# First expert layer as three split products, both slots masked in one instruction, rounding on ScalarE

## The chip, the cores and the metric

The kernel runs on one core of a Trainium2 chip. The metric is the device time of one execution in microseconds (us); of several runs the median counts. The engines are TensorE (PE, matrix products), VectorE (DVE), ScalarE (ACT), GpSimd (POOL) and the DMA queues of SyncE (SP). Each engine works through its own instructions in the order in which they are written; semaphores are all that ties the engines together.

## The reference

Two transformer layers on x of 16 x 128 tokens with 128 features. The first has an attention by autocorrelation and a feed-forward part with composed weights; the second has a plain attention and a mixture of experts. Only the last part is touched by the change:

```
for _ in range(2):                                   # NUM_ITER
    ctx = concat([integrated, v])                    # 256 features
    shared_ctrl = gelu(ctx @ w_s1 + b_s1) @ w_s2 + b_s2
    # each token has K = 2 of E = 8 experts (its slots), with weights flat_w
    hidden = gelu(ctx @ expert_w1[e] + b1[e]);  ctrl = hidden @ expert_w2[e] + b2[e]
    # ctrl -> alpha = sigmoid, beta = softplus, gate = sigmoid; v, x from them
    x_next, v_next = shared weight * shared + rest * sum over the slots
    integrated += sigmoid(halt(x_next)) * refine(x_next) * integration_weight;  v = v_next
```

In the first pass v is zero, so that only the upper half of w1 counts and alpha isn't needed.

## The kernel before

Everything is kept transposed, features on the partitions and 2048 tokens in four chunks of 512 (CH). `build` writes the order of every engine by hand. After the composed weights comes a pipelined stretch of six slots (loop over `t in range(SLOTS)`, on each engine) for feed-forward, attention and router. Its last slot already holds step 0 of the last part: `hidden(0)`, and the masks of its tiles on DVE beside `route(3)`.

Then come eight steps, s = 0 to 7: chunk s % 4, first pass for s < 4, second pass from 4 on. A step has these parts:

- PE, loop at line 1309: `hidden(s+1)` (line 1141), `refine_b(s-2)`, `controls(s, GATE)` and `controls(s, BETA)`, in the second pass ALPHA ahead of them, and `refine_a(s-1)`. In the first pass refine_a comes after BETA, in the second between GATE and BETA. In step 0 the expert numbers (`expand`) and slot weights (`expand_weights`) of chunk 3 are spread through PE too.
- `hidden` makes four tiles of two experts each (128 rows) and the shared tile, as full fp32 products; one product each in the first pass, two (x and v) in the second. The five tiles alternate between two PSUM banks, so tile j waits for the gelu of tile j-2.
- ACT, loop at line 507: `hidden_gelus(s+1)` (line 418), `refine2(s-2)`, then `squashed` (line 495), which is a tanh of 1536 columns for ALPHA and GATE and a softplus for BETA, and `refine1(s-1)` (line 476): two gelus of 512 columns and one of 32 rows. `refine_a` needs the first of these before its 32-column product (`wh1`).
- DVE, loop at line 944: `stepped(s-1)` (line 894), which waits for the softplus of step s-1, `refine(s-2)` (line 928), `hidden_masked(s+1)` (line 761) and `shared_halves(s+1)`.

`hidden_masked` keeps of each tile the columns of the tokens whose slot has that expert, and splits the result in two fp32r halves for the products of `controls`. There are seven masked tiles: the first pair of experts once (`(0, None)`: only one slot can have each of them), and three pairs once for each of the two slots. Per tile it does, on DVE:

```
dve.scalar_tensor_tensor(hm[i % 2], idx[:, c, k, :], W("tile_expert", j, j + 1), hid[:, j, :],
                         ALU.is_equal, ALU.mult)                                  # kept
dve.tensor_copy(out[:, 0, i, :], hm[i % 2])                                       # upper, to fp32r
dve.tensor_tensor(out[:, 1, i, :], hm[i % 2], out[:, 0, i, :].bitcast(F), ALU.subtract)   # lower
```

`controls` is made of fp32r products: upper weights x upper half, lower weights x upper half, upper weights x lower half. The three control parts of the two slots and the shared one fill three of six PSUM banks; the next group but one waits for `squashed`.

Of the kernel before, what the change touches and what calls it, by code (L numbers as in the profile page):

```python
# [1421 lines left out]
```

## Time and profile before

| | before |
|---|---|
| median of 3 runs | 427.25 us (426.93 to 429.09) |
| the profiled execution | 426.0 us, its span 424.2 us |
| PE busy | 354.1 us, 83% |
| DVE busy | 296.2 us, 70% |
| ACT busy | 165.1 us, 39% |
| mean granted clock of PE | 0.947 |
| PE in the chain that ended last | 64% |

The span runs from the first to the last instruction. Times in the rows below are us from its start. A line number of a PE product is that of the helper `mm` (964); the tile names tell which product it is: `xi,pB` and `a,pB` are `hidden` (x and v), `hm_odd,ew_hi` and the like are `controls`, `zz,pB` is `refine_a` and `refine_b`, with `128*32` for its 32-column product. Names of tiles that share memory go by the memory: `zz` is also fh, xn and h1, `kv` is bg, ne and th, `b` is al, `ctxT` is r1, rr and hs, `wz` is hm.

### The profile page before, as it was taken

How to read it: one execution, taken by the hardware profiler on the slowest of the kernel's cores; microseconds unless marked ns; L12 is line 12 of the kernel's file. 1: busy time of each engine (PE TensorE's matmuls, PEld its weight loads, DVE VectorE, ACT ScalarE, POOL GpSimd, SP SyncE). 2: the span in 40 equal slices, each digit the busy share in tenths (PEclk: the TensorE clock that was granted, in tenths of full speed). 3: DMA queues.
4: the chain of work that ended last, by engine and by line, in shares of the span. 5: the costliest groups of instructions: out<-in, count | busy, mean ns of one | idle time of the engine just before them, and what ended most of it. 6: DMA issues, size and time to landing. Idle time of an engine off the chain costs nothing.

```text
span 424.2 us, 4164 instructions
## 1 busy us (share of the span) xinstructions
PE 354.1 (83%) x1406; PEld 207.6 (49%) x1406; DVE 296.2 (70%) x688; ACT 165.1 (39%) x231; POOL 17.0 (4%) x22
## 2 busy tenths in 40 slices
PE   4999997288886684799979899899999999998924
PEld 4646864154553342374626437347537536665511
DVE  0738527757675759998997949939489587866282
ACT  2401226247544465135362533522531452434511
POOL 0200101001100000000000000000000000000000
PEclk9989999879998899699989999999999999999958
DMA  8999230000000000000000000000000000000001
GB/s 268 429 361 300 82 130 0 1 2 0 0 2 0 0 2 0 1 0 2 0 1 2 1 0 0 2 0 0 0 2 1 0 0 26 0 2 25 0 7 42
DMA packets 10724, 17.92 MB, mean 42 GB/s; under 512 B 336, under 2 KB 8528, under 8 KB 9424
## 3 DMA queue, kind: packets, MB, share of 16 engines
q1 hardware_dynamic: 10704, 17.66, 12.2%
q8 instruction: 11, 0.18, 0.2%
q14 instruction: 9, 0.07, 0.1%
HBM read 16.61 MB, written 1.05 MB: 42 GB/s over the span
## 4 chain that ended last, share of the span: by engine, by line
PE 64%; DVE 17%; issue 10%; ACT 5%; POOL 2%; DMA 1%; POOLq 0%; SPq 0%; ACTq 0%; DVEq 0%
PE ps L964 60%; DVE zz L670 3%; DVE lst L655 2%; POOL lrs L319 2%; DMA ctxT<-in_ctxT 1%; PE ps L1047 1%; ACT zz L481 1%; PE ps L1035 1%; DVE hB L759 1%; ACT ctxT L428 1%; DVE st L555 1%; ACT kv L502 1%; DVE lmv L658 1%; DVE a L571 1%; ACT L481 0%
## 5 line engine op out<-in xcount | busy, mean ns | idle before, releaser
L964 PE MATMUL ps<-zz,pB 128*128 128x512 f32 (+2 forms) x96 | 48.8, 624 | 22.3 <-DVE ctxT L933 8.6
L964 PE MATMUL ps<-xi,pB 128*128 128x512 f32 (+1 forms) x88 | 49.6, 672 | 8.2 <-ACT hid L423 4.2
L964 PE MATMUL ps<-hm_even,ew_hi 128*128 128x512 f32 (+1 forms) x160 | 49.1, 418 | 0.0
L964 PE MATMUL ps<-hm_odd,ew_hi 128*128 128x512 f32 (+1 forms) x160 | 48.9, 417 | 0.0
L773 DVE SCALAR_TENSOR_TENSOR wz<-ring,pB,hid 128x512 f32<-128x512 bf16 x56 | 39.8, 746 | 0.3 <-issue 0.2
L964 PEld LDWEIGHTS ps<-zz,pB 128*128 128x128 f32 (+2 forms) x96 | 15.4, 180 | 50.0 <-issue 24.4
L964 PEld LDWEIGHTS ps<-xi,pB 128*128 128x128 f32 (+1 forms) x88 | 15.8, 197 | 32.3 <-ACT hid L423 14.2
L423 ACT ACTIVATE hid<-ps,pB 128x512 f32<-128x512 f32 x32 | 21.8, 687 | 21.6 <-PE ps L964 19.3
L964 PEld LDWEIGHTS ps<-hm_even,ew_hi 128*128 128x128 f32 (+1 forms) x160 | 26.9, 192 | 5.0
L964 PEld LDWEIGHTS ps<-hm_odd,ew_hi 128*128 128x128 f32 (+1 forms) x160 | 26.4, 188 | 5.4
L964 PE MATMUL ps<-hm_even,ew_lo 128*128 128x512 f32 (+1 forms) x80 | 27.6, 393 | 0.0
L964 PE MATMUL ps<-hm_odd,ew_lo 128*128 128x512 f32 (+1 forms) x80 | 27.6, 393 | 0.0
L505 ACT ACTIVATE kv<-ps 128x1536 f32<-128x1536 f32 x8 | 11.6, 1454 | 39.9 <-PE ps L964 39.9
L908 DVE TENSOR_TENSOR kv<-kv 128x1536 f32<-128x1536 f32 x4 | 7.0, 1759 | 28.4 <-ACT kv L502 28.4
L502 ACT ACTIVATE kv<-ps 128x1536 f32<-128x1536 f32 x8 | 11.6, 1452 | 29.3 <-PE ps L964 29.3
L670 DVE TENSOR_SCALAR zz<-ps,lmv,lrs 128x128 f32<-128x128 f32 x48 | 16.4, 404 | 8.4 <-POOL lrs L319 8.2
L655 DVE BATCH_NORM_STATS2 lst<-ps 128x6 f32<-128x128 f32 x48 | 10.7, 285 | 15.6 <-PE ps L1035 15.6
L933 DVE TENSOR_SCALAR ctxT<-ps,pB,iwh 128x512 f32<-128x512 f32 x8 | 6.5, 808 | 20.9 <-PE ps L964 20.9
L964 PE MATMUL ps<-a,pB 128*128 128x512 f32 x40 | 20.4, 592 | 0.0
L783 DVE TENSOR_TENSOR hm_odd<-wz,hm_odd 128x512 fp32r<-128x512 f32 x28 | 18.2, 687 | 0.1
L783 DVE TENSOR_TENSOR hm_even<-wz,hm_even 128x512 fp32r<-128x512 f32 x28 | 18.2, 686 | 0.1
L319 POOL TENSOR_TENSOR lrs<-lve,mhalf 128x4 f32<-128x4 f32 x12 | 12.1, 1007 | 120.8 <-DVE lve L660 120.8
(217 smaller groups left out, 614.3 us busy)
## 6 DMA issues: line engine op xcount, KB each, us to landing
ring<-in_fc1b SPq DMA_DIRECT2D x4, 1024.0 KB, 16.9
ring<-in_fc2a SPq DMA_DIRECT2D x4, 1024.0 KB, 10.0
ring<-in_packC SPq DMA_DIRECT2D x1, 1344.0 KB, 5.7
pB<-in_packB SPq DMA_DIRECT2D x1, 1078.5 KB, 9.9
ctxT<-in_ctxT SPq DMA_DIRECT2D x2, 512.0 KB, 6.4
xtok<-in_xtok SPq DMA_DIRECT2D x1, 1024.0 KB, 9.0
xT<-in_xT SPq DMA_DIRECT2D x1, 1024.0 KB, 11.0
a<-in_fc1a SPq DMA_DIRECT2D x1, 1024.0 KB, 12.9
```

The costliest lines, as they stand in the source:

```text
L319: pool.tensor_tensor(lrs[:, n % 2, :], lve[:, n % 2, :], mhalf[:, 0:BPC], ALU.pow)\
L423: act.activation(hid[:, j, :], hid_bank(s, j), ACT.Gelu, bias=W("eb1", j, j + 1)).then_inc(sem("hid"), 1)
L428: act.activation(hs, hid_bank(s, HT), ACT.Gelu, bias=W("bs1")).then_inc(sem("hs"), 1)
L502: act.activation(bg[:, 0], group_ps(n), ACT.Softplus).then_inc(sem("squash"), 1)
L505: act.activation(out, group_ps(n), ACT.Tanh, scale=0.5).then_inc(sem("squash"), 1)
L655: dve.bn_stats(lst[:, n % 2, j, :], t[:, j * D:(j + 1) * D]).then_inc(sem("lst"), 1)
L670: dve.tensor_scalar(ztok[:, n % 2, j, :], t[:, j * D:(j + 1) * D], lmv[:, n % 2, j, 0:1], lrs[:, n % 2, j:j + 1], ALU.subtract, ALU.mult)\
L773: dve.scalar_tensor_tensor(hm[i % 2], idx[:, c, 2 if k is None else k, :], W("tile_expert", j, j + 1), hid[:, j, :], ALU.is_equal, ALU.mul ...
L783: dve.tensor_tensor(out[:, 1, i, :], hm[i % 2], out[:, 0, i, :].bitcast(F), ALU.subtract).then_inc(sem("hlo"), 1)
L908: link(dve.tensor_tensor(bg[:, 0], bg[:, 0], thrice(ne), ALU.mult))
L933: dve.tensor_scalar(rr, bank[7], W("bf2"), iwh[:, 0:1], ALU.add, ALU.mult).then_inc(sem("rr"), 1)
L964: return pe.matmul(out, lhsT, rhs, start=start, stop=stop)
```

## The change

- `hidden`: each full fp32 product becomes three fp32r products (upper weights x upper state, lower weights x upper state, upper weights x lower state). The halves of w1 are made once in the pipelined stretch, `w1x_hi` on ACT (slot 1), `w1x_lo` on DVE (slot 2). The halves of the state, x and in the second pass v too, are made per step: `state_upper` on ACT, `state_lower` on DVE.
- `hidden_masked`: both slots of tiles 1 to 3 are masked in one instruction of 1024 columns, and their lower halves are made in one of 1024 columns; tile 0 is masked in place, in two instructions of 64 partitions. The copies to fp32r (`upper`) go from DVE to ACT.
- ACT's order: `upper(s+1, ...)` and `state_upper(s+2)` stand between the `squashed` calls of step s, and `upper(0, ...)` and `state_upper(1)` in the last slot ahead of `r1_gelu`.
- `slot_masks` works on the two slots' numbers without copying them first.
- Some tiles move: al, hs, the second hm buffer; w1 stands first in pack B.

The diff, without the lines that only place tiles:

```diff
@@ -419,13 +433,34 @@
...
             if s >= 1:
-                act.wait_ge(sem("hm"), NT * (s - 1) + 2 * j + 1)
+                act.wait_ge(sem("hm") if j else sem("hlo"), HT * (s - 1) + j + 1)
             act.activation(hid[:, j, :], hid_bank(s, j), ACT.Gelu,
...
         act.activation(hs, hid_bank(s, HT), ACT.Gelu, bias=W("bs1")).then_inc(sem("hs"), 1)
+    def upper(s, tiles):
+        for j in tiles:
+            act.wait_ge(sem("hm"), HT * s + j + 1)
+            if s >= 2:
+                act.wait_ge(sem("part_ps"), group(s - 1, 0))
+            out = masked(s)[:, 0, 2 * j - 1:2 * j + 1, :] if j else masked(s)[:, 0, 0, :]
+            act.activation(out, hm[j % 2] if j else hid[:, 0, :], ACT.Copy).then_inc(sem("hhi"), 1)
+    def state_upper(s):
+        c = s % NCH
+        act.wait_ge(sem("hid_ps"), 5 * s)
+        if s >= NCH:
+            act.wait_ge(sem("xi"), c + 1)
+        act.activation(x_hi, xi[:, ck(c)], ACT.Copy).then_inc(sem("xhi"), 1)
+        if s >= NCH:
+            act.wait_ge(sem("v1"), c + 1)
+            act.activation(v_hi, vT[:, ck(c)], ACT.Copy).then_inc(sem("vhi"), 1)
     z_ffn(0)
@@ -460,6 +495,8 @@
...
             act.activation(swc[:, 0:1], W("sw"), ACT.Exp, scale=-1.0).then_inc(sem("swe"), 1)
+            act.activation(w1x_hi, pB[:, colB["ew1"][1]:colB["ew1"][1] + W1C], ACT.Copy)\
+                .then_inc(sem("w1x_hi"), 1)
         if x:
@@ -468,10 +505,18 @@
...
             ln_evac("rt", t - 2, xi[:, ck(t - 2)])
+        if t == 2:
+            act.wait_ge(sem("z"), LN["rt", 0] + 1)
+            act.wait_ge(sem("bp"), 2)
+            act.activation(x_hi, xi[:, ck(0)], ACT.Copy).then_inc(sem("xhi"), 1)
+        if t == SLOTS - 1:
+            upper(0, (0, 1))
+            state_upper(1)
+            upper(0, (2,))
         if q:
...
     second_exp(NCH - 1)
+    upper(0, (3,))
     def refine1(s):
@@ -509,16 +554,24 @@
...
             refine2(s - 2)
+        squashed(s, parts(s)[0])
+        if s + 1 < STEPS:
+            upper(s + 1, (0, 1))
+        if s == 0:
+            expand_evac(NCH - 1, 7, 6)
+        if s + 2 < STEPS:
+            state_upper(s + 2)
+        if s + 1 < STEPS:
+            upper(s + 1, (2,))
+        if s >= NCH:
+            squashed(s, GATE)
+        if s + 1 < STEPS:
+            upper(s + 1, (3,))
         if s < NCH:
-            squashed(s, GATE)
-            if s == 0:
-                expand_evac(NCH - 1, 7, 6)
             squashed(s, BETA)
...
         else:
-            squashed(s, ALPHA)
-            squashed(s, GATE)
             refine1(s - 1)
@@ -747,50 +800,71 @@
...
         dve.wait_ge(sem("idx"), 2 * c + 2)
-        dve.tensor_copy(idx[0:64, c, 2, :], idx[0:64, c, 0, :]).then_inc(sem("idt"), 1)
-        dve.tensor_copy(idx[64:128, c, 2, :], idx[64:128, c, 1, :]).then_inc(sem("idt"), 1)
-        dve.wait_ge(sem("idt"), 2 * c + 2)
-        dve.tensor_scalar(m72[:, ck(c)], idx[:, c, 2, :], W("bias_expert"), None, ALU.is_equal)\
-            .then_inc(sem("m72"), 1)
+        for k in range(2):
+            p = slice(64 * k, 64 * k + 64)
+            dve.tensor_scalar(m72[p, ck(c)], idx[p, c, k, :], W("bias_expert")[p], None, ALU.is_equal)\
+                .then_inc(sem("m72"), 1)
     def slot_weights(c, ba, bb):
...
             dve.tensor_copy(cb[:, c, k, :], bank[(ba, bb)[k]][:, :]).then_inc(sem("cb"), 1)
-    def hidden_masked(s, tiles):
+    def kept(s, j):
         c = s % NCH
+        dve.wait_ge(sem("hid"), HT * s + j + 1)
+        if j == 0:
+            dve.wait_ge(sem("idx"), 2 * (c + 1))
+            for k in range(2):
+                p = slice(64 * k, 64 * k + 64)
+                dve.scalar_tensor_tensor(hid[p, 0, :], idx[p, c, k, :], W("tile_expert", 0, 1)[p],
+                                         hid[p, 0, :], ALU.is_equal, ALU.mult)\
+                    .then_inc(sem("hm" if k else "hm_half"), 1)
+        else:
+            if s >= 1 or j == 3:
+                dve.wait_ge(sem("hlo"), HT * s + (0, -1, 2)[j - 1])
+            dve.scalar_tensor_tensor(hm[j % 2], idx[:, c, :, :], W("tile_expert", j, j + 1),
+                                     hid[:, j, :].unsqueeze(1).to_broadcast([128, 2, CH]),
+                                     ALU.is_equal, ALU.mult).then_inc(sem("hm"), 1)
+    def lower(s, j):
         out = masked(s)
-        n0 = NT * s
-        def kept(i):
-            j, k = TILES[i]
-            dve.wait_ge(sem("hid"), HT * s + j + 1)
-            if n0 + i >= 2:
-                dve.wait_ge(sem("hlo"), n0 + i - 1)
-            dve.scalar_tensor_tensor(hm[i % 2], idx[:, c, 2 if k is None else k, :],
-                                     W("tile_expert", j, j + 1), hid[:, j, :],
-                                     ALU.is_equal, ALU.mult).then_inc(sem("hm"), 1)
-        def upper(i):
-            dve.wait_ge(sem("hm"), n0 + i + 1)
-            dve.tensor_copy(out[:, 0, i, :], hm[i % 2]).then_inc(sem("hhi"), 1)
-        def lower(i):
-            dve.wait_ge(sem("hhi"), n0 + i + 1)
-            dve.tensor_tensor(out[:, 1, i, :], hm[i % 2], out[:, 0, i, :].bitcast(F),
-                              ALU.subtract).then_inc(sem("hlo"), 1)
-        if tiles[0] == 0:
-            dve.wait_ge(sem("idt"), 2 * (c + 1))
-            if s >= 2:
-                dve.wait_ge(sem("part_ps"), group(s - 1, 0))
-        for stage in (kept, upper, lower):
-            for i in tiles:
-                stage(i)
+        dve.wait_ge(sem("hhi"), HT * s + j + 1)
+        if j:
+            i = slice(2 * j - 1, 2 * j + 1)
+            dve.tensor_tensor(out[:, 1, i, :], hm[j % 2], out[:, 0, i, :].bitcast(F), ALU.subtract)\
+                .then_inc(sem("hlo"), 1)
+        else:
+            dve.wait_ge(sem("hm_half"), s + 1)
+            dve.tensor_tensor(out[:, 1, 0, :], hid[:, 0, :], out[:, 0, 0, :].bitcast(F), ALU.subtract)\
+                .then_inc(sem("hlo"), 1)
+    def state_lower(s):
+        c = s % NCH
+        dve.wait_ge(sem("xhi"), s + 1)
+        dve.tensor_tensor(x_lo, xi[:, ck(c)], x_hi.bitcast(F), ALU.subtract).then_inc(sem("xlo"), 1)
+        if s >= NCH:
+            dve.wait_ge(sem("vhi"), c + 1)
+            dve.tensor_tensor(v_lo, vT[:, ck(c)], v_hi.bitcast(F), ALU.subtract)\
+                .then_inc(sem("vlo"), 1)
+    def hidden_masked(s, next_state):
+        kept(s, 0)
+        kept(s, 1)
+        kept(s, 2)
+        if next_state:
+            state_lower(s + 1)
+        lower(s, 0)
+        lower(s, 1)
+        kept(s, 3)
+        lower(s, 2)
+        shared_halves(s)
+        lower(s, 3)
     def shared_halves(s):
@@ -871,24 +945,34 @@
...
             shared_share()
+            dve.wait_ge(sem("w1x_hi"), 1)
+            dve.tensor_tensor(w1x_lo, pB[:, colB["ew1"][1]:colB["ew1"][1] + W1C],
+                              w1x_hi.bitcast(F), ALU.subtract).then_inc(sem("w1x_lo"), 1)
         if a:
...
             slot_weights(t - 3, 2, 3)
+        if t == 3:
+            state_lower(0)
         if f:
...
         if t == SLOTS - 1:
-            hidden_masked(0, (0,))
-            hidden_masked(0, (1, 2))
+            kept(0, 0)
+            kept(0, 1)
+            kept(0, 2)
+            lower(0, 0)
+            lower(0, 1)
         if q:
...
             ln_scale("att", t)
-    hidden_masked(0, (3, 4))
+    state_lower(1)
+    kept(0, 3)
+    lower(0, 2)
     weigh(NCH - 1)
-    hidden_masked(0, (5, 6))
     shared_halves(0)
+    lower(0, 3)
     dve.wait_ge(sem("consts"), 2)
@@ -947,9 +1031,7 @@
...
         if s + 1 < STEPS:
-            for tiles in ((0,), (1, 2), (3, 4), (5, 6)):
-                hidden_masked(s + 1, tiles)
-            shared_halves(s + 1)
+            hidden_masked(s + 1, s + 2 < STEPS)
         if s == 0:
@@ -1141,12 +1223,12 @@
...
         c, it2 = s % NCH, s >= NCH
+        pe.wait_ge(sem("w1x_lo"), 1)
+        pe.wait_ge(sem("xlo"), s + 1)
         if it2:
-            pe.wait_ge(sem("xi"), c + 1)
-            pe.wait_ge(sem("v1"), c + 1)
+            pe.wait_ge(sem("vlo"), c + 1)
         for j in range(HT + 1):
-            name, wd = ("ew1", E * H) if j < HT else ("ws1", 2 * H)
-            o = j * 128 if j < HT else 0
+            o, wd = (j * 128, E * H) if j < HT else (2 * E * H, 2 * H)
             if j >= 2:
@@ -1157,9 +1239,15 @@
...
                     pe.wait_ge(sem("h1"), s - 2)
-            last = mm(hid_bank(s, j), W(name, o, o + 128), xi[:, ck(c)], stop=not it2)
+            out, w = hid_bank(s, j), slice(o, o + 128)
+            mm(out, w1x_hi[:, w], x_hi, stop=False)
+            mm(out, w1x_lo[:, w], x_hi, start=False, stop=False)
+            last = mm(out, w1x_hi[:, w], x_lo, start=False, stop=not it2)
             if it2:
-                last = mm(hid_bank(s, j), W(name, wd + o, wd + o + 128), vT[:, ck(c)], start=False)
+                w = slice(o + wd, o + wd + 128)
+                mm(out, w1x_hi[:, w], v_hi, start=False, stop=False)
+                mm(out, w1x_lo[:, w], v_hi, start=False, stop=False)
+                last = mm(out, w1x_hi[:, w], v_lo, start=False)
             last.then_inc(sem("hid_ps"), 1)
@@ -1256,9 +1344,9 @@
...
             pe.wait_ge(sem("squash"), n - 1)
-        pe.wait_ge(sem("m72"), c + 1)
+        pe.wait_ge(sem("m72"), 2 * (c + 1))
         pe.wait_ge(sem("hsl"), s + 1)
-        pe.wait_ge(sem("hlo"), NT * s + 1)
+        pe.wait_ge(sem("hlo"), HT * s + 1)
         w_hi, w_lo = weights(ew2_hi, 0), weights(ew2_lo, 0)
@@ -1273,7 +1361,7 @@
...
             j, k = TILES[i]
-            pe.wait_ge(sem("hlo"), NT * s + i + 1)
+            pe.wait_ge(sem("hlo"), HT * s + j + 1)
             out = hi if k else lo
```

## Rows read from the trace of the kernel before

**Rows 1.** The page: busy us, share and instructions; granted clock in 40 slices of 10.6 us

```profile
PE 354.1 (83%) x1406; PEld 207.6 (49%) x1406; DVE 296.2 (70%) x688; ACT 165.1 (39%) x231; POOL 17.0 (4%) x22
PEclk9989999879998899699989999999999999999958
```

**Rows 2.** Timeline of PE, step 3: start us, us, line, out<-in, count [idle before]

```profile
257.31 0.39 PE L964 MATMUL ps<-hm_odd,ew_lo 128*128 128x512 f32 x1
...
258.01 0.40 PE L964 MATMUL ps<-hm_odd,ew_lo 128*128 128x512 f32 x1
...
270.38 1.05 PE L964 MATMUL ps<-zz,pB 128*32 128x512 f32 x2 [1.83 <-ACT zz L481]
...
272.31 1.02 PE L964 MATMUL ps<-a,pB 128*128 128x512 f32 x2
273.17 1.02 PE L964 MATMUL ps<-xi,pB 128*128 128x512 f32 x2
```

**Rows 3.** Timeline of ACT, step 3

```profile
260.78 1.46 ACT L505 ACTIVATE kv<-ps 128x1536 f32<-128x1536 f32 x1 [5.42 <-PE ps L964]
262.25 1.28 ACT L502 ACT_TABLE_LOAD   x1
266.87 1.45 ACT L502 ACTIVATE kv<-ps 128x1536 f32<-128x1536 f32 x1 [3.33 <-PE ps L964]
268.34 1.28 ACT L481 ACT_TABLE_LOAD   x1
269.64 1.26 ACT L481 ACTIVATE zz<-ps,pB 128x512 f32<-128x512 f32 x2
```

**Rows 4.** Timeline, step 5: ALPHA's tanh, refine1, the product that waits

```profile
324.22 1.45 ACT L505 ACTIVATE b<-ps 128x1536 f32<-128x1536 f32 x1 [5.41 <-PE ps L964]
...
331.67 1.26 ACT L481 ACTIVATE zz<-ps,pB 128x512 f32<-128x512 f32 x2
...
332.41 1.04 PE L964 MATMUL ps<-zz,pB 128*32 128x512 f32 x2 [0.40 <-ACT zz L481]
```

**Rows 5.** Groups of instructions: busy us, mean ns of one | idle before it

```profile
L423 ACT ACTIVATE hid<-ps,pB 128x512 f32<-128x512 f32 x32 | 21.8, 687 | 21.6 <-PE ps L964 19.3 <-DVE wz L773 2.3
L779 DVE CAST hm_odd<-wz 128x512 fp32r<-128x512 f32 x28 | 10.8, 422 | 0.1
L919 DVE SCALAR_TENSOR_TENSOR kv<-kv,swc 128x1024 f32<-128x1024 f32 x4 | 5.1, 1285 | 0.1
L917 DVE TENSOR_TENSOR kv<-kv,hB 128x1024 f32<-128x1024 f32 x4 | 4.9, 1225 | 0.1
L783 DVE TENSOR_TENSOR hm_odd<-wz,hm_odd 128x512 fp32r<-128x512 f32 x28 | 18.2, 687 | 0.1
L351 ACT ACTIVATE zz<-ps 128x512 f32<-128x512 f32 x4 | 2.4, 596 | 13.5 <-PE ps L1047 13.5
```

**Rows 6.** Timeline, step 0: ACT, DVE's slot weights, PE's hidden(2)

```profile
184.75 1.45 ACT L505 ACTIVATE kv<-ps 128x1536 f32<-128x1536 f32 x1 [7.00 <-PE ps L964]
186.10 1.08 ACT L415 ACTIVATE ring<-ps 128x512 bf16<-128x512 f32 x2
...
192.07 1.29 DVE L759 COPY hB<-ps 128x512 f32<-128x512 f32 x2 [1.44 <-PE ps L1137]
...
193.41 4.93 PE L964 MATMUL ps<-xi,pB 128*128 128x512 f32 x10 [0.95 <-DVE hB L759]
```

**Rows 7.** Timeline, slot 5: r1_gelu, start of route(3), first controls

```profile
161.15 0.68 ACT L400 ACTIVATE ctxT<-ps,pB 32x512 f32<-32x512 f32 x1 [1.14 <-PE ps L964]
...
164.81 0.18 DVE L714 COPY lg<-ps 128x32 f32<-128x32 f32 x1
...
177.07 0.39 PE L964 MATMUL ps<-xtok,bp_e 64*128 64x512 bf16 x2 [2.54 <-issue]
```

**Rows 8.** Timeline of PE at the end: the same six records twice

```profile
410.52 4.42 PE L964 MATMUL ps<-zz,pB 128*128 128x512 f32 x6 [8.56 <-DVE ctxT L933]
415.80 3.01 PE L964 MATMUL ps<-zz,pB 128*128 128x512 f32 x6 [0.86 <-ACT zz L486]
```

More of the change, by code:

```diff
@@ L33 @@
 VG = -(-B // VB)
-PACK_B = [("wq", 128, D), ("wo", 128, D), ("bq", 128, 1), ("bv", 128, 1), ("bo", 128, 1),
+PACK_B = [("ew1", 128, 2 * E * H), ("ws1", 128, 4 * H), ("wq", 128, D), ("wo", 128, D), ("bq", 128, 1), ("bv", 128, 1), ("bo", 128, 1),
           ("wr1", 128, 32), ("br1", 32, 1), ("wr2", 33, E), ("wh1", 128, 32), ("bh1", 32, 1),
-          ("wh2", 32, 1), ("bh2", 128, 1), ("ew1", 128, 2 * E * H), ("eb1", 128, HT),
-          ("ws1", 128, 4 * H), ("bs1", 128, 1), ("wf1", 128, 2 * D), ("bf1", 128, 2),
+          ("wh2", 32, 1), ("bh2", 128, 1), ("eb1", 128, HT), ("bs1", 128, 1), ("wf1", 128, 2 * D), ("bf1", 128, 2),
           ("wf2", 128, 2 * D), ("bf2", 128, 1), ("iw", 128, 1), ("mu", 128, 1), ("sw", 128, 1),
@@ L71, in sem @@
             return sems[name]
+        xtok_at = (nc.sbuf_base + 31) // 32 * 32
         xtok_f = sb("xtok", [128, B * D])
@@ L78, in build @@
         ctxT = sb("ctxT", [128, T])
+        pA_at = (nc.sbuf_base + 31) // 32 * 32
         pA = sb("pA", [128, nA])
+        pB_at = (nc.sbuf_base + 31) // 32 * 32
         pB = sb("pB", [128, nB])
         a1_f = sb("a1", [128, KC * D])
+        b2_at = (nc.sbuf_base + 31) // 32 * 32
         b2_f = sb("b2", [128, KC * D])
@@ L184, in C @@
             return ring[0:r, PC0 + at:PC0 + at + n]
-        idx = ring[:, IDX0:IDX0 + 3 * T // 2].bitcast(BF).rearrange("p (c a n) -> p c a n", c=NCH, a=3)
+        idx = ring[:, IDX0:IDX0 + T].bitcast(BF).rearrange("p (c a n) -> p c a n", c=NCH, a=2)
         m72 = xtok_f[:, 0:T // 2].bitcast(BF)
@@ L200, in build @@
         hid = hid_f[:, :].rearrange("p (f n) -> p f n", f=HT)
-        hs = ctxT[:, 2 * CH:3 * CH]
+        hs = wz[:, 2 * CH:3 * CH]
         hsh = sb("hsh", [128, 2, CH], FR)
-        hm = (wz[:, 0:CH], wz[:, CH:2 * CH])
+        hm = (wz[:, 0:2 * CH].rearrange("p (k n) -> p k n", k=2),
+              ring[:, IDX0 + T:IDX0 + T + 2 * CH].rearrange("p (k n) -> p k n", k=2))
         hm_even = sb("hm_even", [128, 2, NT, CH], FR)
@@ L209, in build, with placed @@
         ws2_lo = sb("ws2_lo", [128, 3 * D], FR)
+        W1C = 2 * E * H + 4 * H
+        def placed(name, cols, at):
+            return nc.alloc_sbuf_tensor_at(name, [128, cols], FR, offset=at)[:, :]
+        w1x_hi = placed("w1x_hi", W1C, b2_at)
+        w1x_lo = placed("w1x_lo", W1C, pB_at + 4 * colB["ew1"][1])
+        x_hi, x_lo = (placed(n, CH, xtok_at + 4 * (2 + i) * CH) for i, n in enumerate(("x_hi", "x_lo")))
+        v_hi, v_lo = placed("v_hi", CH, b2_at + 4 * W1C), placed("v_lo", CH, pA_at)
         bg = kv[:, 0:6 * CH].rearrange("p (a k n) -> p a k n", a=2, k=3)
@@ L213, in build @@
         th = kv[:, 7 * CH:8 * CH]
-        al = b2_f[:, 0:3 * CH].rearrange("p (k n) -> p k n", k=3)
+        al = ctxT[:, 0:3 * CH].rearrange("p (k n) -> p k n", k=3)
         fh = zz[:, 0:2 * CH].rearrange("p (f n) -> p f n", f=2)
```

## The prediction

> **What bounds the kernel now.** I read the page first: TensorE (PE) is busy 83% of the span, and its granted clock is low only in a few slices [rows 1]. The chain of waits gives PE 64% of the span. Then I read the timelines from 177 us on, where the eight steps of the last layer run. Step s issues, on PE, hidden(s+1), refine_b(s-2), one `controls` group per part, and refine_a(s-1) ahead of the last group (after it in steps 0 to 3). All of it is back to back, except for a short stop per step. In step 3 the GATE group ends near 260.75 and the BETA group at 266.8. PE finishes the first half of refine_a and stops for 1.83 us, until 270.38 [rows 2]. It waits there for ScalarE (ACT): softplus 266.87, table load, gelu 269.64 [rows 3]. The table load ahead of that softplus (262.25) costs nothing: it runs while PE does the BETA group. So a step is PE work plus a short tail through ACT. VectorE (DVE) makes the masked halves one step ahead and ends them before they are needed.
>
> **Gain on PE.** A full fp32 product is two records of 0.43 us start to start, 0.86 us together (272.31 to 273.17) [rows 2]. Three fp32r products take 258.01 - 257.31 = 0.70 us [rows 2]. So hidden() falls by 0.16 us per product set, 5 sets in steps of the first pass and 10 in those of the second: at most 4 x 0.8 + 4 x 1.6 = 9.6 us. It can't all be had: two PSUM banks alternate, so tile j waits for the gelu of tile j-2, 0.69 us each [rows 5].
> - hidden(2): five tiles at 0.86 took 4.87 before the next group. Now tiles 2 to 4 go at the gelu's pace, 4.0 in all: gain 0.87. hidden(3): 0.4, for its end waits for the last gelu.
> - hidden(4), hidden(5): 1.4 us a tile, start to refine_b 9.72 before, 7.95 after: 1.77 each.
> - hidden(6), hidden(7): the first gelu stands behind a softplus and a table load, so tile 2 starts at 3.7 us in both kernels; three tiles by 0.3: 0.92 each.
> Sum 6.65 us.
>
> **The copies on ScalarE, first pass (steps 1, 2, 3).** DVE loses seven casts of 0.42 us a step [rows 5] (and gets state_lower, 0.69 or 1.4), but DVE isn't the bound. What matters is the place of the copies in ACT's order. `upper(s+1)` stands between squashed(s, GATE) and squashed(s, BETA), and upper(s+1, 3) waits for kept(s+1, 3). That waits for lower(s+1, 1) (same buffer), which waits for upper(s+1, 1); and DVE has state_lower(s+2) in front of it, which waits for ACT's copy of the state. So ACT and DVE pass the work to and fro, and softplus is queued behind it. From the end of the GATE group, in us:
> - tanh done 1.5 [rows 3]; upper 0 (512 columns, 0.60) 2.1; upper 1 (1024 columns, halfway between the 596 ns of 512 and the 1.46 us of 1536, so 1.03) 3.15; x_hi 3.75 [rows 3, 5];
> - DVE: x_lo 0.69, lower 0 0.70, lower 1 (1024 columns, 1225 ns), kept 3 (1024 columns, 1285 ns), each with 0.03 to 0.1 between: 7.83 [rows 5];
> - ACT: upper 3 8.9, table load 1.28, softplus 1.46: 11.7; table load for gelu, gelu 0.69: 13.75.
> Before, the product behind that gelu started 270.38 - 260.75 = 9.63 us after the GATE group. The load that used to be free is exposed as well. Step 1: +4.1. Steps 2 and 3 make the state of the second pass, with v_lo (0.70) in the DVE part: +4.8 each. DVE's own kept 0 to 2 are done before the tanh ends, so they don't lengthen this.
>
> **Step 0.** Here hidden(2) waited for DVE's slot weights, 193.41 - 184.7 = 8.7 us after the GATE group [rows 6]. Now ACT has tanh, upper 0 and 1 (3.15), two index evictions (1.09) and x_hi before DVE can go on (4.85); DVE then has x_lo, lower 0, lower 1, kept 3, lower 2, shared halves (1.18), lower 3, the masks (0.65) and the slot weights (1.29): 14.55. That is +5.85.
>
> **Second pass (steps 4 to 6).** From the end of ALPHA: tanh 1.5, upper 0 and 1 3.15, x_hi 3.75; DVE x_lo, v_lo, lower 0, lower 1, kept 3: 8.5; upper 3 9.6; gelu of refine1 10.3. Before, that gelu released PE at 332.41 - 324.18 = 8.23 [rows 4]. So +2.1 in steps 4 and 5. Step 6 makes no state: kept 3 at 5.8, the GATE tanh done at 7.55, upper 3 8.6, gelu 9.3: +1.1. Step 7 has no masked work: 0. BETA's table load stays behind refine1, where it was.
>
> **Prologue.** Slot 2 puts w1x_lo (1280 columns, 1.5 us by the slope of DVE's rows) and slot 3 x_lo (0.7) on DVE; part goes into its idle time, and the index copies left out give a little back: I take 0.9. ACT's copies of w1 and x stand where it waits for PE anyway: nothing, or 1.8 us if that cover were gone. In slot 5 r1_gelu, which ended at 161.83, comes after upper 0, upper 1, x_hi(1) and upper 2, and ends at 165.85; with router2's 1.0 behind it route(3) starts at 166.9, not 164.81 [rows 7]. It takes 2.85, then x_lo(1) 0.7: hidden(1) starts at 170.5. Upper(0, 3) is done at 172.8, the gelu load at 174.1, and the tiles go at the gelu's pace; the last ends at 177.2, or 178.7 at half the clock, in the middle 178.0. With the 0.9 the first group starts at 178.9, not 177.07 [rows 7]: +1.8. Bounds: -1, if DVE's shorter list tells in the end, and +4, if all of r1_gelu's delay stays.
>
> **The clock.** The tail's stop on PE grows from 1.83 to about 5.9 us in steps 1 to 3, and to 6.5 us in step 0. No row shows a stop of just that length. Where PE had stood idle for 8.6 us, six records took 4.42 us; the same six took 3.01 us five us later [rows 8], and the page's clock row falls to 5 in that slice [rows 1]: 1.2 GHz for part of it, against 2.4. After stops of 1.83 us the clock stays high in most steps. So I bound it: nothing, or 5.0 us a stop (12 us of PE work at the low clock before it is back); I take 2.0, near the row. Four stops, 8 us; the clock digit 8 in the slice of 212 to 223 says that the kernel before already pays about 2 us in hidden(3) [rows 1]. Net +6, bounds 0 and +18.
> The Trainium skill (TensorE: Matmul & The Clock Gate, What's actually happening) says of a model that it may leave the ramp out, as under 1% of a typical span. By it the sum would be without this term, the second rival below. The row of the 8.6 us stop speaks for a cost of 1.4 us each, so the sum keeps the term.
>
> **Sum.** 1.8 + 5.85 + 4.1 + 4.8 + 4.8 + 2.1 + 2.1 + 1.1 - 6.65 = +20.0, and the clock +6: +26. The profiled execution took 426.0 us with a span of 424.2, so it would take 452.0 with a span of 450. It lies 1.25 us under the median of the runs, 427.25; I predict 453.0 for the median.
>
> **Unknown costs.** ACT's copy of 1024 columns from SBUF has no row: not under 0.60 (512 columns), not over 1.46 (1536). Two stand in each chain (uppers 1 and 3): -0.9 to +0.9 a step. DVE's masked instruction of 1024 columns with a bf16 and a repeated operand: 0.75 (one of 512) to 1.76 (1536 columns), taken by the same form at 1024 (1285 ns): -0.5 to +0.5. Over seven steps -9.5 to +9.5 together at the ends.
>
> **Rivals.**
> 1. PE stays the bound (the other side): if ACT reached the copies early enough for kept 3 to be done within the 6.1 us of the last group, the tail would be hidden as now and only the 6.65 us of hidden() would show: 427.25 - 6.65 + 1.8 = 422.4. For it: ACT is busy 39% and DVE 70% of the span [rows 1], and the work moved is small. Against: the chain after the tanh is 7.4 us on two in-order engines, over 6.1; it decides only from a chain 1.3 us shorter, and then the table load would also have to go ahead of upper 3.
> 2. The tail grows, the clock holds through stops of 6 us: 427.25 + 20 = 447.
> 3. The tail grows, and the clock stays at 1.2 GHz for much of the first pass, 5 us lost at each of four stops: 427.25 + 20 + 18 = 465.
> 4. The tail grows by half of what I say, as when DVE and ACT copies come at the low ends: 427.25 + 10 + 2 = 439.
> 5. No change: the 6.65 us and a tail of that size cancel, 427.
>
> **Chances.** Forecast 0.50, rival 2 0.20, rival 3 0.08, rival 4 0.14, rival 1 0.05, rival 5 0.03. The range 440 to 463 holds the forecast, rival 2 and the near part of 4 and 3. A change of 0.5% (2.1 us) is about what a measurement here can tell. Faster 0.05, same 0.03, slower 0.92.
>
> **What would show it.** In the profile after, ACT's softplus in steps 1 to 3 stands right behind a copy of 1024 columns and a table load, 10 us and more after the tanh; the PE stop ahead of the 32-column product is near 6 us in steps 1 to 3 and near 2.6 in steps 4 and 5; hidden(4) goes from 9.7 to 8.0 us; the clock falls after the long stops. It is wrong if softplus still starts within 0.1 us of the BETA group's end, or if those stops stay under 3 us.

## The result and the profile after

| | before | after |
|---|---|---|
| median | 427.1 us (426.2 to 429.1, 4 runs) | 451.3 us (450.2 to 453.1, 4 runs) |
| ratio after to before, 95% interval | | 1.056 (1.051 to 1.061) |
| profiled execution, its span | 426.0, 424.2 us | 451.9, 450.0 us |
| mean granted clock of PE | 0.947 | 0.917 |
| PE in the chain that ended last | 64% | 52% |

The kernel is 24.2 us slower. The forecast was 453.0, and for the profiled execution 452.0 with a span of 450.

The page after, the same lines as in [rows 1], in slices of 11.25 us:

```profile
PE 353.3 (79%) x1466; PEld 225.6 (50%) x1466; DVE 287.3 (64%) x601; ACT 200.4 (45%) x276; POOL 17.0 (4%) x22
PEclk9999999699987895988969889979999999999968
PE 52%; DVE 22%; issue 11%; ACT 10%; POOL 2%; DMA 1%; POOLq 0%; ACTq 0%; SPq 0%; DVEq 0%
```

PE has as many busy microseconds as before, although its products became shorter: part of them ran at a lower clock. DVE has 9 us less work and ACT 35 us more, and neither is close to full. What is new is waiting.

Timeline of ACT in step 2 after (start us, us; the idle time ahead in brackets). It answers to [rows 3]; steps 1 and 3 have the same order (step 1 without the copy of v):

```profile
244.28 1.45 ACT L550 ACTIVATE kv<-ps 128x1536 f32<-128x1536 f32 x1 [5.31 <-PE ps L1046]
245.63 0.62 ACT L452 ACTIVATE hm_odd<-hid 128x512 fp32r<-128x512 f32 x1
246.15 1.05 ACT L452 ACTIVATE hm_odd<-ring 128x1024 fp32r<-128x1024 f32 x1
247.10 0.62 ACT L460 ACTIVATE x_hi<-xi 128x512 fp32r<-128x512 f32 x1
247.62 0.62 ACT L463 ACTIVATE v_hi<-a 128x512 fp32r<-128x512 f32 x1
248.14 1.05 ACT L452 ACTIVATE hm_odd<-wz 128x1024 fp32r<-128x1024 f32 x1
252.20 1.06 ACT L452 ACTIVATE hm_odd<-ring 128x1024 fp32r<-128x1024 f32 x1 [3.01 <-DVE ring L828]
253.28 1.28 ACT L547 ACT_TABLE_LOAD   x1
254.57 1.45 ACT L547 ACTIVATE kv<-ps 128x1536 f32<-128x1536 f32 x1
256.04 1.28 ACT L526 ACT_TABLE_LOAD   x1
257.34 1.27 ACT L526 ACTIVATE zz<-ps,pB 128x512 f32<-128x512 f32 x2
```

And DVE in the same stretch:

```profile
247.75 0.69 DVE L849 TENSOR_TENSOR x_lo<-xi,x_hi 128x512 fp32r<-128x512 f32 x1 [3.30 <-ACT x_hi L460]
248.36 0.68 DVE L852 TENSOR_TENSOR v_lo<-a,v_hi 128x512 fp32r<-128x512 f32 x1
248.96 0.68 DVE L842 TENSOR_TENSOR hm_odd<-hid,hm_odd 128x512 fp32r<-128x512 f32 x1
249.56 1.22 DVE L838 TENSOR_TENSOR hm_odd<-ring,hm_odd 128x1024 fp32r<-128x1024 f32 x1
250.89 1.28 DVE L828 SCALAR_TENSOR_TENSOR ring<-ring,pB,hid 128x1024 f32<-128x1024 bf16 x1
```

The ball goes over twice. DVE stands idle for 3.30 us until ACT has copied the state. Then ACT stands idle for 3.01 us until DVE has masked tile 3 (the instruction at 250.89). Only behind the last copy does ACT come to the softplus, and now the load of its table (253.28) stands on the path; in [rows 3] the same load was done 3.3 us ahead of its softplus, beside PE's work.

Timeline of PE behind that gelu, which answers to [rows 2]:

```profile
258.08 1.91 PE L1046 MATMUL ps<-zz,pB 128*32 128x512 f32 x2 [6.10 <-ACT zz L526]
...
260.51 0.63 PE L1046 MATMUL ps<-x_hi,w1x_lo 128*128 128x512 f32 x1
260.94 0.63 PE L1046 MATMUL ps<-x_lo,w1x_hi 128*128 128x512 f32 x1
...
265.20 0.40 PE L1046 MATMUL ps<-v_hi,w1x_lo 128*128 128x512 f32 x1
265.43 0.40 PE L1046 MATMUL ps<-v_lo,w1x_hi 128*128 128x512 f32 x1
```

The stop is 6.10 us instead of 1.83; in steps 1 and 3 it is 5.43 and 6.02. Behind it two products take 1.91 us, not 1.05 [rows 2], and the products of `hidden` start 0.43 us apart instead of 0.23: the lower of the clock's two levels (1.2 GHz against 2.4; the granted clock is 0.50 from 257 to 262 us and 1.00 from 264 on), until some 5 us after the stop.

Step 0, start of hidden(2), and the end of the kernel, which answer to [rows 6, 8]:

```profile
201.64 0.77 PE L1046 MATMUL ps<-x_hi,w1x_hi 128*128 128x512 f32 x1 [6.11 <-DVE hB L811]
...
322.40 1.05 PE L1046 MATMUL ps<-zz,pB 128*32 128x512 f32 x2 [1.92 <-ACT zz L526]
...
435.20 5.58 PE L1046 MATMUL ps<-zz,pB 128*128 128x512 f32 x6 [8.56 <-DVE ctxT L1017]
```

In step 0 PE stops for 6.11 us instead of 0.95. The first stop of the second pass (322.40) is 1.92 us; those behind it are 1.84 and 1.35, and all three were 0.40 [rows 4].

### The profile page after: what moved, and what is told of

Same layout as the page of the kernel before. It is cut to its first block, busy times and chain, and to the rows that moved or that the text cites. A ratio compares the mean times of both kernels' runs of the same rounds, so it can differ in the third digit from the quotient of the medians.

```text
span 450.0 us, 4256 instructions
## 1 busy us (share of the span) xinstructions
PE 353.3 (79%) x1466; PEld 225.6 (50%) x1466; DVE 287.3 (64%) x601; ACT 200.4 (45%) x276; POOL 17.0 (4%) x22
## 3 DMA queue, kind: packets, MB, share of 16 engines
HBM read 16.61 MB, written 1.05 MB: 39 GB/s over the span
## 4 chain that ended last, share of the span: by engine, by line
PE 52%; DVE 22%; issue 11%; ACT 10%; POOL 2%; DMA 1%; POOLq 0%; ACTq 0%; SPq 0%; DVEq 0%
PE ps L1046 49%; DVE zz L723 2%; DVE ring L828 2%; DVE lst L708 2%; POOL lrs L333 2%; ACT hm_even L452 2%; DVE hm_odd L838 1%; DMA ctxT<-in_ctxT 1%; ACT hm_odd L452 1%; PE ps L1129 1%; ACT zz L526 1%; ACT hid L437 1%; PE ps L1117 1%; ACT L526 1%; ACT L547 1%
## 5 line engine op out<-in xcount | busy, mean ns | idle before, releaser
L1046 PE MATMUL ps<-zz,pB 128*128 128x512 f32 (+2 forms) x96 | 52.5, 665 | 38.3 <-ACT zz L526 24.5
L1046 PE MATMUL ps<-x_hi,w1x_hi 128*128 128x512 f32 x40 | 20.2, 506 | 13.0 <-DVE hB L811 6.1
L550 ACT ACTIVATE kv<-ps 128x1536 f32<-128x1536 f32 x8 | 11.6, 1453 | 28.9 <-PE ps L1046 28.9
L1046 PEld LDWEIGHTS ps<-x_hi,w1x_hi 128*128 128x128 f32 x40 | 9.0, 225 | 24.3 <-issue 15.1
L828 DVE SCALAR_TENSOR_TENSOR ring<-ring,pB,hid 128x1024 f32<-128x1024 bf16 x16 | 20.5, 1283 | 1.0
L849 DVE TENSOR_TENSOR x_lo<-xi,x_hi 128x512 fp32r<-128x512 f32 x8 | 5.5, 691 | 24.3 <-ACT x_hi L460 24.2
L708 DVE BATCH_NORM_STATS2 lst<-ps 128x6 f32<-128x128 f32 x48 | 10.6, 284 | 15.4 <-PE ps L1117 15.3
L547 ACT ACTIVATE kv<-ps 128x1536 f32<-128x1536 f32 x8 | 11.6, 1452 | 16.3 <-PE ps L1046 16.3
L1046 PE MATMUL ps<-x_hi,w1x_lo 128*128 128x512 f32 x40 | 18.1, 451 | 0.0
L1046 PE MATMUL ps<-x_lo,w1x_hi 128*128 128x512 f32 x40 | 17.8, 446 | 0.0
```

Source lines behind the costliest of these rows:

```text
L547: act.activation(bg[:, 0], group_ps(n), ACT.Softplus).then_inc(sem("squash"), 1)
L550: act.activation(out, group_ps(n), ACT.Tanh, scale=0.5).then_inc(sem("squash"), 1)
L708: dve.bn_stats(lst[:, n % 2, j, :], t[:, j * D:(j + 1) * D]).then_inc(sem("lst"), 1)
L828: dve.scalar_tensor_tensor(hm[j % 2], idx[:, c, :, :], W("tile_expert", j, j + 1), hid[:, j, :].unsqueeze(1).to_broadcast([128, 2, CH]), A ...
L1046: return pe.matmul(out, lhsT, rhs, start=start, stop=stop)
```

## The experiments

The kernel before ran beside each, with a median of 427.3 us beside e1 to e4 and 427.2 beside e5 to e8. A ratio is to it, with its 95% interval. Where two kernels are compared that both differ from it by little (e1, e2, e5, e8), the uncertainties of both ratios count.

| what is run | median us | ratio | span, clock of the profile |
|---|---|---|---|
| e1: copies back on DVE | 425.7 | 0.994 (0.990 to 0.997) | 421.2, 0.943 |
| e3: one copy later in ACT's order | 431.9 | 1.012 (1.008 to 1.015) | 429.8, 0.934 |
| e4: full products again, copies on ACT | 444.4 | 1.037 (1.032 to 1.042) | 444.2, 0.930 |
| e8: wide masks alone | 426.1 | 0.997 (0.994 to 1.000) | 423.5, 0.952 |
| e2: e1 with masks per slot | 430.0 | 1.004 (1.001 to 1.007) | 429.0, 0.926 |
| e6: PE kept busy through the stops | 443.3 | 1.034 (1.028 to 1.041) | 442.4, 0.942 |
| e7: tanh in place of softplus | 439.7 | 1.026 (1.020 to 1.032) | 438.8, 0.916 |
| e5: copies on DVE, step 0 reordered | 421.9 | 0.988 (0.983 to 0.992) | 420.0, 0.944 |

### The copies back on DVE (e1)

```diff
-def upper(s, tiles):                          # on ACT, with state_upper, among the squashed calls
...
-    act.activation(out, hm[j % 2] if j else hid[:, 0, :], ACT.Copy)
+def upper(s, j):                              # on DVE, in hidden_masked, with state_upper
...
+    dve.tensor_copy(out, hm[j % 2] if j else hid[:, 0, :])
```

> The changed kernel with all copies to fp32r of the masked tiles and of the state on DVE again (ScalarE keeps only the one of w1). Theory (the tail of each step is ScalarE's copies and DVE's lowers passed to and fro ahead of softplus and of refine1's gelu): the tails go back to those before, PE's stops ahead of the 32-column product to 1.8 us in steps 1 to 3 and 0.4 in 4 to 6, the clock drops after them are gone, and the 6.65 us of hidden() show: 427 - 6.7 + 2 to 3 in the pipelined stretch = 423, 420 to 426. Rival (the split products or the double-width masks themselves cost the time, on PE or DVE): it stays near 450. Rival (DVE becomes the bound, for it gets 1.1 to 2.0 us more a step than in the kernel before): 430 to 435.

It took 425.7 us: all 24 us are gone, and 1.6 more. The product behind the gelu, in steps 1 to 3:

```profile
217.88 1.04 PE L1045 MATMUL ps<-zz,pB 128*32 128x512 f32 x2 [1.83 <-ACT zz L497]
242.74 1.04 PE L1045 MATMUL ps<-zz,pB 128*32 128x512 f32 x2 [1.83 <-ACT zz L497]
270.58 1.05 PE L1045 MATMUL ps<-zz,pB 128*32 128x512 f32 x2 [1.83 <-ACT zz L497]
```

The stop is again 1.83 us and the granted clock stays at 1.00 behind all three, with DVE busy 73% instead of 64%. So the whole loss goes when one part of the change is taken back, the move of the rounding to ACT.

### One copy later in ACT's order (e3)

```diff
-                if s + 1 < STEPS:
-                    upper(s + 1, (3,))
                 if s < NCH:
                     squashed(s, BETA)
-                    if s >= 1:
-                        refine1(s - 1)
-                else:
+                if s >= 1:
                     refine1(s - 1)
+                if s + 1 < STEPS:
+                    upper(s + 1, (3,))
+                if s >= NCH:
                     squashed(s, BETA)
```

> The changed kernel with one thing moved: upper(s+1, 3) stands behind squashed(s, BETA) and refine1(s-1) in the first pass, and behind refine1(s-1) in the second, with all the same work on ScalarE. Theory (the order, not the amount): tails of steps 1 to 6 go back to about the ones before; step 0 keeps some 3 us and the pipelined stretch its 3 us: 427 - 6.65 + 6 = 427, 423 to 432. Rival (the amount of work on ScalarE): 445 or more.

431.9 us: 19.4 of the 24.2 us come back, with the same work on ACT. ACT in step 2:

```profile
242.87 1.05 ACT L452 ACTIVATE hm_odd<-wz 128x1024 fp32r<-128x1024 f32 x1
243.94 1.28 ACT L547 ACT_TABLE_LOAD   x1
245.24 1.45 ACT L547 ACTIVATE kv<-ps 128x1536 f32<-128x1536 f32 x1
246.71 1.28 ACT L526 ACT_TABLE_LOAD   x1
248.00 1.27 ACT L526 ACTIVATE zz<-ps,pB 128x512 f32<-128x512 f32 x2
249.82 0.68 ACT L531 ACTIVATE zz<-ps,pB 32x512 f32<-32x512 f32 x1 [0.56 <-PE ps L1045]
250.41 1.04 ACT L452 ACTIVATE hm_odd<-ring 128x1024 fp32r<-128x1024 f32 x1
```

The copy that waited 3.01 us now stands behind refine1, and no stop of PE waits for it. The stops on PE are 1.82, 2.04 and 1.96 us, and 0.40 in the second pass. Only step 0 keeps its cost: hidden(2) still starts behind a stop of 6.11 us, at 201.39. There the expectation was off (3 us were to remain of the start), for of step 0 only upper(1, 3) was moved. The other copies still stand ahead of the index evictions and of x_hi, and DVE's slot weights behind x_lo.

### Full products with the copies on ACT (e4), and wide masks alone (e8)

```diff
...
-    mm(out, w1x_hi[:, w], x_hi, stop=False)
-    mm(out, w1x_lo[:, w], x_hi, start=False, stop=False)
-    last = mm(out, w1x_hi[:, w], x_lo, start=False, stop=not it2)
+    last = mm(hid_bank(s, j), W(name, o, o + 128), xi[:, ck(c)], stop=not it2)
...
```

and no `state_upper` or `state_lower`. e8 is e4 with the copies on DVE, as in e1: of the change it keeps only the new masks (1024 columns for tiles 1 to 3, tile 0 in place) and `slot_masks` without its copies.

> The changed kernel with hidden() made of full fp32 products as before; the halves of w1 and of the state aren't made. Masks, copies on ScalarE and their place stay. Theory: hidden() costs its 6.65 us again, but the chain of each tail is 1.1 us (x) or 1.7 to 2.2 us (x and v) shorter; the tail of steps 1 to 3 is still 2 to 3 us over the one before and PE's stop 4 to 4.5 us: 447, 441 to 451. Rival (the split products are what costs): back at 427.

> Only the double-width masks of the change: hidden() with full fp32 products, copies on DVE, no halves of w1 or of the state. Theory: DVE's work isn't on the path of the steps, and tile 0 in two instructions gives back what the width saves; only slot 5, where DVE is behind, can tell: 426, 424 to 428. Against e1_round_dve (425.7) it tells what the split products alone are worth there: hidden()'s 6.65 us less what their halves cost in slots 2 to 5 and in step 0. Rival: the masks' width is worth 3 us or more, and this one is at 423 or below.

e4 took 444.4. Without x_hi and v_hi on ACT and x_lo and v_lo on DVE the chain is 1.7 to 2.3 us shorter (stops of 3.70, 3.79 and 3.71 us), the stop ahead of hidden(2) is 3.32 us instead of 6.11, and the clock costs less behind them. Together that is worth more than the shorter products: the split products cost 6.9 us net in the order of the change (451.3 against 444.4).

e8 took 426.1, against 425.7 of e1. So the wide masks alone give about 1 us (by the interval 0.1 to 2.8), and the split products nothing that can be told in e1's order: there hidden(2) starts at 197.7 us and in e8 at 191.7. 3.7 of these 6.0 us are there at hidden(0) already (156.3 against 152.6, partly the clock, see e2); the other 2.3 come in slot 5 and step 0, where DVE makes the halves of the state ahead of the slot weights of chunk 3.

### Masks per slot (e2)

```diff
-dve.scalar_tensor_tensor(hm[j % 2], idx[:, c, :, :], ..., hid[:, j, :].unsqueeze(1).to_broadcast([128, 2, CH]), ...)
+for k in range(2):
+    dve.scalar_tensor_tensor(hm[j % 2][:, k, :], idx[:, c, k, :], ..., hid[:, j, :], ...)
```

The same for the copies and the lower halves.

> As e1_round_dve, but tiles 1 to 3 are masked, copied and lowered per slot in instructions of 512 columns (18 instead of 9 a step). By the durations a 1024-column mask saves 0.2 us against two of 512 start to start (1.20 against 1.32), all nine about 0.5 us a step, in DVE's slack: theory: same as e1 within 1 us (423). Rival (the width of the masks matters): 3 us or more over e1.

430.0, or 4.3 us over e1: the expectation of no difference was wrong. Not all of it can be placed. The two profiles lie 7.8 us apart. 2.7 of that is there at the start of hidden(0) already (159.0 against 156.3), and a kernel whose instructions up to there are those of "after" (e7) also starts it at 158.5, against 155.6 of "after": that much comes and goes with the granted clock before 155 us. In slot 5 and step 0, where PE waits for DVE, the shift grows by 1.6 us up to hidden(2), which waits 4.00 us instead of 3.15, and the clock falls behind it: 5.3 us at the product ahead of hidden(3). In e2 the clock falls once more behind the stop of 1.83 us in step 2, which adds 1.5, and the last 0.9 come at the last products. The tails of the steps are the same in both, 1.83 and 0.40 us. So only the 1.6 us, and the 1.0 of the clock behind them, stand where the narrower instructions are on the path; how much of the 4.3 us of the medians is theirs stays open.

### PE kept busy (e6)

```diff
+def keep_busy(n, count):
+    pe.wait_ge(sem("squash"), n + 1)
+    for _ in range(count):
+        mm(bank[3 * (n % 2)], onesb[:, 0:128], onesb[:, :])
```

Called ahead of the wait for the gelu in steps 1 to 3, and in step 0 ahead of hidden(2).

> The changed kernel with 24 bf16 products of 512 columns on PE, into a bank that is free, in the long stop of each of steps 0 to 3 (some 5.2 us of work in stops of 5.4 to 6.1 us); their results aren't used. Theory (the stops also cost clock): the granted clock stays at 2.4 GHz after them, the 32-column product takes 1.05 us for two records as before and not 1.92, hidden()'s products follow each other in 0.23 us and not 0.43: 2.0 to 2.6 us less per stop, four stops: 451.3 - 9 = 442, 440 to 445. Rival (the clock term is nothing, and the loss is all in the chain): 450 to 452.

443.3. PE in the stop of step 2, with the 24 unused products:

```profile
248.37 5.34 PE L1046 MATMUL ps<-onesb 128*128 128x512 bf16 x24
254.64 1.04 PE L1046 MATMUL ps<-zz,pB 128*32 128x512 f32 x2 [0.93 <-ACT zz L526]
255.61 0.50 PE L1046 MATMUL ps<-x_hi,w1x_hi 128*128 128x512 f32 x1
255.95 0.40 PE L1046 MATMUL ps<-x_hi,w1x_lo 128*128 128x512 f32 x1
256.19 0.40 PE L1046 MATMUL ps<-x_lo,w1x_hi 128*128 128x512 f32 x1
```

Nothing that the kernel needs comes sooner in the chain on ACT and DVE, but the two products take 1.04 us and those of `hidden` start 0.23 apart: the clock is high behind the stop. From the end of each stop to the end of its `hidden`, e6 takes 1.2, 2.3, 2.3 and 2.2 us less than the kernel after (hidden(2) to hidden(5)): 8.1 us for the clock behind the four stops. What else differs between the two profiles nearly cancels: in step 4 of e6 the clock falls behind a stop of 1.92 us, which costs 1.6, and the last products take 1.2 less. The medians lie 8.0 us apart, a third of the loss of 24.2; the rest is what the longer stops themselves and the prologue cost, less what the split products give.

### The tables (e7)

```diff
-act.activation(bg[:, 0], group_ps(n), ACT.Softplus)
+act.activation(bg[:, 0], group_ps(n), ACT.Tanh)
```

> The changed kernel with tanh in the place of softplus for BETA, which changes the values of beta. ScalarE then has no table load before it nor behind it. Theory (the load that was hidden now stands in the tail): in steps 1 to 3 both loads (1.28 us each) leave the chain of upper 3, load, softplus, load, gelu: PE's stop shrinks from 6 to 3.4 us, 2.6 us less each, and with shorter stops some of the clock's loss goes: 451.3 - 7.8 - 4 = 440, 435 to 444. In step 0 and the second pass nothing changes. Rival (the loads run beside the copies and cost nothing): 448 or more.

With tanh beta has other values, so only the time of this kernel is of use: 439.7, or 11.6 us less. In step 2 ACT goes on without a gap:

```profile
250.13 1.06 ACT L452 ACTIVATE hm_odd<-ring 128x1024 fp32r<-128x1024 f32 x1 [3.01 <-DVE ring L828]
251.09 1.43 ACT L547 ACTIVATE kv<-ps 128x1536 f32<-128x1536 f32 x1
252.42 1.26 ACT L526 ACTIVATE zz<-ps,pB 128x512 f32<-128x512 f32 x2
```

ACT still waits 3.01 us for DVE, and the stops shrink to 2.58, 3.26 and 3.18 us. Two loads of 1.28 us stand on the path of each of those steps in the kernel after; one of them did before. The loads also leave places that the expectation took as unchanged: the stop in step 7 goes from 1.82 to 0.40 us, and hidden(6) and hidden(7) are 1.0 us shorter each. The profile of e7 reaches the first tanh of step 0 3.0 us later than that of the kernel after, so it tells the differences only from there on.

### The version to keep (e5)

From e1, these calls moved in slot 5 and step 0:

```diff
+            if t == SLOTS - 1:                     # ACT: the copy of x for hidden(1)
+                act.wait_ge(sem("hid_ps"), 5)
+                act.activation(x_hi, xi[:, ck(1)], ACT.Copy).then_inc(sem("xhi"), 1)
...
-                    upper(0, 0)                    # DVE, slot 5: now behind route(3)
-                    upper(0, 1)
-                    lower(0, 0)
-                    lower(0, 1)
+                    state_lower(1)
...
+                if s == 1:                         # DVE, ahead of shared_halves(1)
+                    slot_masks(NCH - 1)
+                    slot_weights(NCH - 1, 7, 6)
```

and `shared_halves(0)` goes ahead, `weigh(3)` behind the lower halves.

> e1_round_dve with its slot 5 and step 0 put in another order: ScalarE makes x_hi(1) where it was idle, DVE does x_lo(1) and route(3) ahead of the upper and lower halves of step 0, shared_halves(0) ahead of tile 3, weigh(3) last, and slot masks and weights of chunk 3 stand ahead of shared_halves(1). In e1 PE stopped 7.6 us ahead of hidden(1) and 3.2 us ahead of hidden(2). Theory: e1 still has 4.3 us of the change's cost at the start of hidden(2) (197.7 against 193.4 in the kernel before), and it goes, with a little more: GATE of step 0 near 176, hidden(2) near 192: 425.7 - 5.7 = 420, 417 to 423, faster than both kernels. Rival: the pipelined stretch is bound by its clock and DVE in another place, and it stays at 424 to 427.

421.9 us, 5.2 under the kernel before beside it. Against e1 the medians differ by 3.7 us and the ratios by 2.6, with an interval that just reaches 0. hidden(2) starts at 194.8, not at 197.7 (192 was expected):

```profile
194.81 0.47 PE L1047 MATMUL ps<-x_hi,w1x_hi 128*128 128x512 f32 x1 [2.18 <-DVE hB L777]
```

Behind this stop the clock falls (from 195.4 to 198.9 us), which it doesn't in e1, so that the product ahead of hidden(3) is 2.0 us sooner than in e1. e5 beats both kernels, the one before by 0.8 to 1.7%. It is also 4.2 us under e8. But e8 has its slot 5 and step 0 in the old order, and no run has full products in the order of e5: how much of the 4.2 us the split products give and how much the order isn't shown.

## Why the prediction was right

The direction, the place and the mechanism hold: the copies among ACT's calls lengthen PE's stops, and e3 and e1 take that loss back. The sum lands within 2 us: 453.0 forecast, 451.3 measured; +26 forecast between the profiles, +25.8 measured. That it lands so near is partly luck, for its terms are off by up to 3.7 us and cancel. The steps one by one, from the starts of the same instructions in the two profiles:

- **The chain, steps 1 to 3.** Forecast +4.1, +4.8, +4.8; measured +3.6, +4.3, +4.2. In step 2 the GATE group ends near 244.25. Kept 3 is done 7.9 us later (8.5 by the terms with v_lo), upper 3 9.0, softplus 11.8, gelu 13.8 (9.6, 12.4, 14.4). The order is exactly the forecast one. The 0.6 us are in how the terms were added: I put 0.03 to 0.1 us between instructions of one engine, and behind one another they start 0.05 to 0.1 us before the earlier one's recorded end (ACT's copies of 0.62 and 1.05 us start 0.52 and 0.95 apart). The unknown cost was right: the copy of 1024 columns took 1.05 us (1.03 taken), the masked instruction 1.28 (1.285 taken). e3 is the test of the mechanism: one copy moved, 19.4 us back.
- **Step 0.** +5.85 forecast, +5.2 measured, the same small error. DVE waits 7.53 us for x_hi there, behind the two index evictions, as forecast.
- **Steps 4 to 6.** +2.1, +2.1, +1.1 forecast; +1.5, +1.4, +0.9 measured. With step 0 and steps 1 to 3 the stops cost 21.1 us where 24.85 were forecast.
- **hidden().** -6.65 forecast for the products at the high clock. Measured at the high clock it is 6.1: hidden(2) and hidden(3) gain 0.5 each (4.36 us in e6 against 4.87 before; 6.27 in e6 against 6.78 in e8, which has full products), hidden(4) and hidden(5) 1.6 each (9.11 in e6 against 10.69 before), hidden(6) and hidden(7) 0.94 and 0.95 in the kernel after itself. In the kernel after, hidden(2) to hidden(5) don't show it, for they stand behind a stop: they take 0.73, 0.30, 0.73 and 0.62 us more than before. So one of the signs that the prediction named did not come: hidden(4) went from 9.7 to 9.6 us, not to 8.0.
- **The clock.** 8 us forecast for four stops, less some 2 that the kernel before pays already, net +6. Measured 8.1 for the four stops (e6), less 1.5 (hidden(3) with the product ahead of it took 8.29 us before, where the clock falls, and 6.78 in e8, where it doesn't): net +6.6. This term was right. Its upper bound of 5.0 us a stop has no row behind it, and the dearest cost 2.3 in the kernel after and 2.9 in any run (e7, step 2: 12.03 us for the product and hidden(4), against 9.11 in e6). Not in the forecast is the last group of six products: it takes 5.58 us instead of 4.42 [rows 8] behind a stop of 8.56 us that both kernels have, 1.2 more; e2 and e3 have 5.60 there, e4 4.45, so this is no effect of the change that could be shown. The rival in which the clock holds (447) is out, both by e6 and by the rows at 260.51. The Trainium skill (TensorE: Matmul & The Clock Gate, What's actually happening) puts the ramp penalty at under 1% of a typical kernel span. For one stop the trace agrees, 2.0 us or 0.45% of the span of 450.0; for the four together, which is what the second rival leaves out, it doesn't: 8.1 us, 1.8%.
- **The prologue.** +1.8 forecast, +3.1 measured at the first tanh of step 0 (187.82 against 184.75), within the bounds of -1 and +4. r1_gelu ended at 169.2, not 165.85 as forecast from [rows 7]. Where it comes from depends on the execution: "after" starts hidden(0) 3.3 us later than before with a granted clock of 0.80 from 120 to 155 us, while e3 and e6, which have the same instructions up to there, start it 1.0 and 1.3 us later at 0.90 and lose the rest in slot 5. The first tanh stands 2.8 to 3.2 us later in these three and 6.0 in e7. So the term was too small by 1.3 us, and one profile can't tell it better than to a few us.

The sum of the misses: 3.7 us too much for the stops, against 1.3 too little for the prologue, 0.6 each for the clock and for `hidden`, and 1.2 at the last products.

The rivals: the chain never came under the 6.1 us of PE's last group, so PE did not stay the bound (422 forecast for it). The nearest run to that case is e1, where the copies left ACT: it has the stops of before and took 425.7, for slot 5 and step 0 still cost time there; with those in another order (e5) it is 421.9. Half the tail (439) is out by the stops of 5.4 to 6.1 us.

What I had not weighed is that the order of one copy decides. The prediction speaks of the place of the copies in ACT's order but not of the question whether another place would do; e3 shows that it would, down to 431.9, and e1 and e5 that the place on DVE is better still.

## What to carry to other kernels

Before a small operation moves to the engine that has idle time, write down what that engine's next instructions are and whom they release: one copy that waits for another engine, put ahead of an activation that PE needs, cost 19 us of 451 on an engine that was busy 45% of the span. Put such an operation behind the last instruction of the step that somebody waits for. A table load that costs nothing is free only as long as its activation stands next in line while the engine waits; an instruction that waits, put between them, makes the load visible. And count the clock with a stop: here four longer stops cost 8.1 us in clock on top of the 21.1 us of waiting in all steps.

## What the runs showed of the hardware

- **Stops and the clock.** In the ten traces, from the first tanh of step 0 on, the granted clock fell to 0.50 in or just behind 6 of 36 stops of 1.8 to 2.6 us, 7 of 8 stops of 3.1 to 4.0 us (not that of 3.15 us in e1) and all 6 of 5.4 to 6.1 us. The product behind the stop doesn't tell it: in e4 it took 1.05 us behind 3.70 us of stop and 1.91 behind 3.79, and the clock fell both times, the first time 1 us later. So the ten products of `hidden` must be read with it. e4 behind a stop of 3.70 us, and e8, where the clock held:

```profile
224.06 1.05 PE L1009 MATMUL ps<-zz,pB 128*32 128x512 f32 x2 [3.70 <-ACT zz L509]
225.04 6.44 PE L1009 MATMUL ps<-xi,pB 128*128 128x512 f32 x10
...
213.84 1.04 PE L1007 MATMUL ps<-zz,pB 128*32 128x512 f32 x2 [1.83 <-ACT zz L495]
214.82 4.93 PE L1007 MATMUL ps<-xi,pB 128*128 128x512 f32 x10
```

Such a fall cost 1.5 us here, and 2.2 to 2.3 behind the stops of 5.4 to 6.1 us in steps 1 to 3 of the kernel after. The kernel before has the same 6.44 us in step 1 (215.07), behind a stop of 1.83 us.
- **ACT and DVE on the same copy.** From fp32 to fp32r, 512 columns: 0.62 us on ACT and 0.42 on DVE; 1024 columns: 1.05 on ACT and 0.69 on DVE (e1). So the move also made each copy longer.
- **Half the partitions save nothing.** Groups of DVE after (busy us, mean ns of one); the first is the mask of tile 0, for which the kernel before took 746 ns with 128 partitions:

```profile
L821 DVE SCALAR_TENSOR_TENSOR hid<-ring,pB,hid 64x512 f32<-64x512 bf16 x16 | 11.9, 744 | 0.3
L877 DVE TENSOR_TENSOR hsh<-wz,hsh 64x512 fp32r<-64x512 f32 x8 | 5.5, 690 | 0.3
L842 DVE TENSOR_TENSOR hm_odd<-hid,hm_odd 128x512 fp32r<-128x512 f32 x4 | 2.7, 686 | 1.1 <-ACT hm_odd L452 1.1
```

Masking tile 0 in two instructions of 64 partitions thus costs twice what one of 128 did (1.52 us for the two in step 0).
